# A language-model tower layer on one core: first choice behind the scores, evictions ahead of the exponentials in routing groups, and unused products on TensorE

## The reference

```python
h = concat(emb_table[ids], interp(|stft(onehot(ids))|) @ proj_w.T + proj_b)   # (2, 2048, 256)
x = layernorm(h)
Q, K, V = x @ Wq + bq, x @ Wk + bk, x @ Wv + bv
p = softmax(Q . K[i-2 .. i+2] / sqrt(256), masked at the ends)
h = h + sum(p * V[i-2 .. i+2])
x = layernorm(h)
probs = softmax(x @ router_w + router_b)       # 8 experts
top2, weights = top_k(probs, 2), normalised
rank of each (token, choice) in its expert; kept where rank < cap (1280)
eo = gelu(x @ w1[e] + b1[e]) @ w2[e] + b2[e]   # 256 -> 512 -> 256, the kept rows of each expert
h = h + sum over the two choices of weight * eo
```

## Time and profile before

| | us |
|---|---|
| median of 3 runs | 380.99 |
| lowest, highest | 379.92, 382.88 |
| the profiled execution | 382.53 |
| its span, first to last instruction | 380.7 |
| PE busy | 326.0 (86%) |
| DVE busy | 259.0 (68%) |
| ACT busy | 209.2 (55%) |
| POOL busy | 205.0 (54%) |
| mean granted TensorE clock | 0.942 of full |

### The profile page before, as it was taken

One profiled execution on the slowest core, in us unless ns is written; L12 is line 12 of the kernel. 1 busy time (PEld: TensorE's weight loads), 2 busy tenths in 40 slices (PEclk: granted clock), 3 DMA queues, 4 the chain that ended last, 5 costly groups with the idle time before them and its releaser, 6 DMA issues.

```text
span 380.7 us, 9114 instructions
## 1 busy us (share of the span) xinstructions
PE 326.0 (86%) x2616; PEld 269.0 (71%) x2616; DVE 259.0 (68%) x836; ACT 209.2 (55%) x481; POOL 205.0 (54%) x156
## 2 busy tenths in 40 slices
PE   0689998987978969596999779999999999999970
PEld 0646767665756647374888558888888888888860
DVE  4955456579887986898676457667667677676650
ACT  1634794687869764662455335555555555555530
POOL 5015460000575775777787644584856555655761
PEclk9999996899889975989899999999999999999996
DMA  6999778795273444948499877686978668644552
GB/s 136 322 306 382 240 271 359 300 401 199 84 266 129 157 151 126 220 145 201 132 131 179 139 115 101 103 105 94 130 102 116 86 102 122 102 43 56 58 57 28
DMA packets 82268, 61.85 MB, mean 162 GB/s; under 512 B 55843, under 2 KB 75844, under 8 KB 80780
## 3 DMA queue, kind: packets, MB, share of 16 engines
q1 hardware_dynamic: 68462, 42.64, 42.1%
q0 software_dynamic: 13760, 18.63, 28.2%
HBM read 15.75 MB, written 35.27 MB: 134 GB/s over the span
## 4 chain that ended last, share of the span: by engine, by line
PE 57%; DVE 15%; DMA 14%; issue 4%; ACT 3%; SPq 3%; POOL 2%; POOLq 0%; ACTq 0%; DVEq 0%
PE bank L1691 22%; PE bank L1678 21%; DMA inv_rows<-reg_a 6%; DMA reg_a<-inv_rows 4%; DMA out<-reg_h,meta 3%; PE bank L1572 3%; PE bank L1574 2%; POOL out L593 2%; SPq L471 1%; PE bank L1387 1%; PE bank L1558 1%; DVE reg_a L852 1%; DVE reg_h L1323 1%; PE bank L1398 1%; DVE reg_z L1250 1%
## 5 line engine op out<-in xcount | busy, mean ns | idle before, releaser
L593 POOL DMA_INDIRECT out<-reg_h,meta x74 | 115.9, 1566 | 68.2 <-DMA out<-reg_h,meta 31.9
L1678 PE MATMUL bank<-reg_z,w1s 128*128 128x256 f16 (+1 forms) x936 | 111.9, 269 | 4.6 <-ACT reg_a L792 3.8
L1691 PE MATMUL bank<-w2s,reg_h 128*128 x888 | 111.0, 276 | 2.8 <-DVE reg_h L1323 2.8
L572 POOL DMA_INDIRECT slot_rows<-reg_z,slots x64 | 66.5, 1039 | 68.2 <-DVE reg_z L1250 51.2
L1678 PEld LDWEIGHTS bank<-reg_z,w1s 128*128 x936 | 88.7, 99 | 16.8 <-issue 5.8
L1691 PEld LDWEIGHTS bank<-w2s,reg_h 128*128 128x128 f16 x888 | 87.1, 99 | 14.8 <-issue 3.9
L792 ACT ACTIVATE reg_a<-bank,b1s 128x256 f32<-128x256 f32 (+1 forms) x156 | 70.3, 463 | 30.9 <-PE bank L1678 27.4
L804 ACT ACTIVATE reg_h<-bank,meta 128x256 f32<-128x256 f32 x74 | 35.1, 474 | 72.5 <-PE bank L1691 65.0
L1329 DVE SCALAR_TENSOR_TENSOR reg_h<-reg_w,meta,reg_h 128x256 f32<-128x256 f32 x74 | 35.9, 485 | 48.4 <-ACT reg_h L804 46.0
L1323 DVE SCALAR_TENSOR_TENSOR reg_h<-reg_a,reg_h 128x256 f16<-128x256 f32 (+1 forms) x156 | 64.7, 415 | 5.4
L1321 DVE TENSOR_SCALAR reg_h<-reg_a 128x256 f16<-128x256 f32 (+1 forms) x156 | 46.7, 299 | 9.7 <-ACT reg_a L792 7.0
(11 more groups left out here) (231 smaller groups left out, 359.7 us busy)
## 6 DMA issues: line engine op xcount, KB each, us to landing
slot_rows<-reg_z SPq DMA_DIRECT2D x8, 1360.0 KB, 9.2
reg_h<-w SPq DMA_DIRECT2D x12, 512.0 KB, 9.3
out<-reg_p SPq DMA_DIRECT2D x8, 512.0 KB, 3.3
reg_w<-w SPq DMA_DIRECT2D x4, 512.0 KB, 10.8
out<-reg_z SPq DMA_DIRECT2D x1, 1280.0 KB, 15.4
out<-reg_h,meta POOLq DMA_INDIRECT x74
reg_a<-inv_rows SPq DMA_DIRECT2D x6, 193.5 KB
reg_a<-masks SPq DMA_DIRECT2D x1, 1056.0 KB, 11.2
```

The source lines that it names most:

```text
L572: nc.gpsimd.indirect_dma_start(out=slot_rows, out_offset=bass.IndirectOffsetOnAxis(ap=slots[:, side, n:n + 1], axis=0), in_=x2w[:, n % RIN ...
L593: nc.gpsimd.indirect_dma_start(out=out.rearrange("t p c -> (t p) c"), out_offset=bass.IndirectOffsetOnAxis(ap=meta[:, p, s, 0:1], axis=0), ...
L1678: last = mm(bank[(0, 2, 3)[n % 3]][:, 0:rows_of(p)], w1s[:, wp, bass.ds(expert[p], 1), kt, j * P:(j + 1) * P].rearrange("p e c -> p (e c)" ...
L1691: last = mm(bank[4 + n % 4][:, 0:H], hT[:, p % 2, hp, f, s * P:(s + 1) * P], w2s[:, wp, bass.ds(expert[p], 1), f, :].rearrange("p e c -> p ...
```

## The change

Seven edits:

1. VectorE's `first_choice(c)` goes from the end of `attend(g)` to `attend(g + 1)`, behind `scores(g + 2)` and ahead of `normed(g + 3)`.
2. `order_early()` is split: its first step, which reads TensorE's totals, stays behind group 5 (`read_totals`), the 11 others go to group 6, behind `first_choice`.
3. In routing groups ScalarE evicts tiles 0 and 1 first, then takes exponentials and evictions in turn, and the last two exponentials at the end.
4. ScalarE's `copy_g(1)` goes ahead of `pair_high(11)` and `copy_prT(0)`.
5. TensorE's `scores(1)` goes from `attend(0)` to the setup, ahead of `turn_values()`.
6. From group 2 on, TensorE does five products that nobody reads (128x256, 16 bit, into bank 3) ahead of the turn of the probabilities.
7. `rank(3)` and `count_late()` go from behind `layer1(1, 0)` to behind `layer1(1, 1)`, with sixteen unused products (bank 7) ahead of them.

```diff
@@ ScalarE, attend(g)
-                    for t in range(TPG):
-                        exps(g + 1, t)
-                        evict(g, t)
+                    if ended(g - 1):
+                        evict(g, 0)
+                        evict(g, 1)
+                        exps(g + 1, 0)
+                        evict(g, 2)
+                        exps(g + 1, 1)
+                        evict(g, 3)
+                        exps(g + 1, 2)
+                        exps(g + 1, 3)
+                    else:
+                        for t in range(TPG):
+                            exps(g + 1, t)
+                            evict(g, t)
@@ ScalarE, setup
             copy_ut(0)
+            copy_g(1)
             pair_high(11)
             copy_prT(0)
-            copy_g(1)
@@ VectorE
-            def order_early():
+            def read_totals():
 
                 have = totals.unsqueeze(2).to_broadcast([NU, E, UPE])
                 dve.wait_ge(totals_done, 1)
                 tt(under.rearrange("u (e j) -> u e j", j=UPE), have, of_units(C_FULL), ALU.is_ge).then_inc(totals_read, 1)
+
+            def order_early():
+
                 dve.wait_ge(totals_read, 1)
...
                 if more:
                     scores(g + 1)
+                for c in ended(g - 1):
+                    first_choice(c)
                 if more2:
                     normed(g + 2)
+                if g == 6:
+                    order_early()
                 for c in ended(g - 1):
                     second_choice(c)
...
                 if g == 5:
-                    order_early()
+                    read_totals()
                 for c in ended(g):
                     deviation(c)
-                    first_choice(c)
@@ TensorE
+            def keep_busy(bk, count):
+
+                for _ in range(count):
+                    mm(bk[:, 0:H], con[:, 0:P // 2].bitcast(F16), con[:, 0:P].bitcast(F16), start=True, stop=True)
+
             def turn_probs(g):
 
+                if g > 1:
+                    pe.wait_ge(prT_ready, g)
+                    keep_busy(bank[3], 5)
...
                 if g:
                     mix(g)
-                if more:
+                if g and more:
                     scores(g + 1)
...
             turn_probs(0)
+            scores(1)
             turn_values()
...
-                    if (p, j) == (1, 0):
+                    if (p, j) == (1, 1):
+                        keep_busy(bank[7], 16)
                         rank(len(CHUNKS) - 1)
                         count_late()
```

## The result

| | before | changed |
|---|---|---|
| median, us | 381.4 (4 runs) | 385.31 (4 runs) |
| lowest, highest | 379.92, 382.88 | 384.72, 385.89 |
| the profiled execution | 382.53 | 384.72 |
| its span | 380.7 | 382.9 |
| mean granted clock | 0.942 | 0.939 |

The ratio on record, formed from each kernel's fast executions (those within 1.5% of its fastest), is 1.0151, 95% interval 1.0093 to 1.0208; the two medians alone give 1.010. In these runs the changed kernel is slower, and 385.31 lies above the stated range of 375.0 to 383.5. 12 executions of it in a later comparison gave 383.09, which lies inside that range, and 1.0037 (0.9971 to 1.0104), which can't be told from no change. So the loss is somewhere between nothing and 1.5%; in neither is the forecast of 380.0 us reached.

A forecast was written before the change was run, and what follows sets the result against it. The end moves only by what both chains gain: chunk 2's slots with GpSimd, and TensorE. Terms -2.3 + 0.2 + 1.3 + 0.3 + 0.1 - 0.6 = -1.0 us, set on the 380.99 median: 380.0 us, range 375.0 to 383.5.

The forecast's parts named there:

- for the other groups 0: Clock in groups 3 to 6: no net change expected, total idle time unchanged; ends at -1.9 and +3.3 us.
- one long wait: Rival: idle gathered ahead of turns in groups 2 and 4 slows groups 3 and 5; sum +5.3, 386.3 us; chance 0.10.
- nothing but the shift: Rival: clock falls in the front as before, which gives 1.0 instead of 2.3; sum +0.3, 381.3 us; chance 0.20.
- Front, -2.3: Setup: group 1's scores fill TensorE's idle gap ahead of the value table's transposes; 2.3 us gained, bounds 1.0 and 3.6.
- Group 2, +0.2: First choice behind the scores: VectorE's masking waits about 0.2 us for TensorE's scores; TensorE's total idle stays the same.
- groups 5 and 6, +0.3: Sorting steps and first choice now stand behind the masking, which waits some 0.3 us for TensorE.
- Evictions first in group 4, +1.3: Two exponentials follow the last eviction, ending about 117.45; 1.3 us lost on VectorE's chain, whatever the clock.
- Five products, +0.1: Unused products ahead of turns take 0.55 us, 1.1 at lower clock, mostly fitting idle time; +0.1 us in all.
- Turn of group 7, -0.6: Turn of group 7, ranks and list: half the chance of full clock; -0.6 us, range 0 to -1.2.
- Last ranks, 0: Edit 7 fits TensorE's 3.79 us wait for the counts; VectorE's work hides any gain, so 0.
- The bound that I described: GpSimd: chunk 2's rows can start earlier only by 2.53 us plus chunk 1's shift; as rival 380.5, chance 0.05.
- same: Outcome within about 1% (3.8 us) of the kernel before; given 0.67, against 0.23 for faster and 0.10 for slower.

The follow-up runs named there:

- the filled waits: Changed kernel with 25, 19, 38 unused products ahead of turns 3, 5, 7: 379.55 us, 0.999; with edit 3 undone and 25, 5, 38: 377.99, 0.992; again 376.39, 0.9898.
- the two traces with a slow residual above: Changed kernel with waits filled (379.55 us, 0.999), and the repeat of it with edit 3 undone (376.39 us, 0.9898); group 4's residual is slow in both.
- the unfilled kernels: Five products at each turn: the changed kernel measured again (383.09 us, 1.0037) and the changed kernel with edit 3 undone (384.49 us, 1.0135).
- The filled kernels in the old order of evictions: Changed kernel with edit 3 undone and 25, 5 and 38 unused products ahead of turns 3, 5 and 7: 377.99 us, 0.992; again 376.39 us, 0.9898.
- the filled new order: Changed kernel with edit 3 undone and 25, 5, 38 unused products: 377.99 us, beside the kernel before with edits 4 and 5 alone, 377.55 us.

## Why the prediction was wrong

**The step that failed** is the clock's term in the sum: "for the other groups 0", because "the total idle time is unchanged". In the traces compared, groups 3 and 5 together took 4.15 us more (1.58 and 2.57), with 6.8 us at the lower level in group 3 for 3.4 and 6.8 in group 5 for none. The premise did not hold either: without products TensorE's wait in group 2 is 3.08 us for 1.08 and 1.34, and ahead of turn 7 it is 4.24 for 3.16 and 0.26, so the total rose as it was gathered into one piece. Which of the two matters, the length of the piece or the total, no run separates. That TensorE's standing still there is what costs, the filled waits show. I had the upper end of +3.3 for it in the sum and the mechanism among the rivals, "one long wait", and gave that 0.10. It is the case that came in the first comparison; in the second, 1.0037 doesn't tell it from "nothing but the shift". Two of the signs that I had named came: gaps of VectorE between 117 and 139 (1.13 us at 122.28, 0.85 at 126.91), and GpSimd's first row of chunk 2 0.68 later where I had it 1 earlier.

Its price of +5.3, 386.3 us, looks close to the measured median of 385.31, but part of that is luck. In the traces the change costs 2.2 us. Of these 1.6 are the low stretch at 226 us, which is not shown to be the change's. In the other direction 1.84 came back in group 4, where I had priced a loss of 1.3: the transfer of the biases was hardly waited for, and its wait, which had been there before, took up what was late ahead of it. Had that come as priced and the stretch at 226 stayed away, the sum would have been some 3.7. Group 3 cost 1.58 instead of 3.3, group 5 2.57 for about 3.

What spoke for that rival in the trace of before was more than 0.10, and I used it only in one direction. In group 7 the level was low for 11 of 12 us behind a wait of 3.16 us at 136.56. In group 3, with two waits of 1.08 and 1.34, it was low for 3.4. A change that makes group 2's waits look like group 6's should have been given a good chance of group 7's clock. One trace could not have settled it: behind the same two waits another had 10.3 us.

**The other steps.**

*Front, -2.3.* Right in these two traces. VectorE starts the factors of group 1's probabilities at 69.45 for 71.77, 2.32 earlier, and the router tables end at 62.57 for 64.36, which is the full clock until there that I chose between the bounds. Over the traces of all runs turn 1 comes between 67.98 and 70.72 us with the edits (16 traces) and at 67.10, 72.81, 72.89 and 73.03 without: mostly a clear gain, but the one at 67.10, with the old order and only 3.4 us of lower level in the setup, is ahead of all that have the edits. The clock moves this point by more than the edits do.

*Group 2, +0.2, and groups 5 and 6, +0.3.* Near enough. From turn 2 to turn 3 it takes 11.88 for 11.50, +0.38, and from turn 6 to turn 7 12.91 for 12.77, +0.14. From turn 1 to turn 2 it takes 0.37 more, which the sum did not have.

*Evictions first in group 4, +1.3.* Not paid in the profiled execution, since it rested on the late biases, which were no longer late. Where they are late, it is paid: the exponentials are done 1.9 us later, and the turn comes 1.6 later, in the two traces with a slow residual above. I had said that it "does not depend on the clock". It does: at the lower level the last two exponentials wait for the last slow residual, and 1.9 is more than 1.3. On the unfilled kernels it does not show: 1.0037 with it, 1.0135 without, which I can't explain beyond the differing places at which the clock fell (43.7 and 51.1 us at the lower level).

*Five products, +0.1.* Their length was right: 16 take 1.91 us and 25 take 2.89, 0.109 for each one more, 0.55 for five. They leave 2.53 of the 3.07 us in the long wait.

*Turn of group 7, -0.6.* Near: from the turn to the mixing behind it it takes 2.02 us for 2.48. Only the turn itself is at full clock, since it falls at 141.5; ranks and list run at the lower level as before, and the stretch behind is low until 151.7. And the turn had begun 1.11 late.

*Last ranks, 0.* Right. They wait 1.17 us for the counts instead of 3.79, and the end doesn't know of it.

*GpSimd.* The bound that I described is the one that a filled kernel met in one of four traces. The filled kernels in the old order of evictions gained 0.8 and 1.0%.

The chance of 0.67 for "same" and the lower end of 375.0 rested on a clock that gets no worse. The page that I cited from the Trainium skill ("TensorE: Matmul & The Clock Gate", PE-mode transpose) spoke for the slower case in routing groups, since by its rule transposes don't count as products do, and the stretch of turn, wait and turn gets longer there. The result agrees with that direction; whether transposes count could not be told, since in the filled kernels (full clock, 1.00 from 90 to 104 us) it was the idle time that was replaced, and the transposes stayed.

## What to carry to other kernels

Where TensorE waits in mid-kernel, look at what stands behind the wait. Moving work so that short waits become one long one ahead of products can cost more than the order gains, because the work behind it can run at half speed for longer (3.4 to 13.7 us of it here). If the order needs the long wait, fill it whole with products that nobody reads: 5 where 25 fit did little, 25 held the clock. And compare the result with leaving the order alone: here the filled new order was only level with the old one.

## What I had not expected

- One program, one chip: the kernel before spreads from 375.85 to 387.63 us over 29 executions, and its span goes with the mean granted clock (correlation -0.74 to -0.89 in the quiet comparisons). A profile is one draw from this; differences below 2 us between two traces have to be followed to a row or left.
- A single low stretch in the experts can cost in full. 3.4 us of it at 226 us put 1.6 us on the end, three times the 0.54 that was lost up to 212 us. Another of 3.4 us at 213, ahead of a wait of 1.78 us, cost next to nothing.
- The transfer of the biases lands so that ScalarE waits 0.21 to 3.68 us for it, from kernel to kernel and run to run, with 1,024 KB each time; where ScalarE comes later still, it waits for nothing. It is a part of whether the way from turn 4 to turn 5 takes 11.7 us (0.21 waited) or 13.5 (2.06), but the clock is another: with 1.27 us waited and full clock it took 11.71, with 1.64 and a slow residual 14.65.
